# A one-core AdaLN attention and MoE-LoRA block: VectorE's rsqrt of the second FFN half's rows taken apart over units, row statistics ahead of row scalings, two mask banks exchanged

## What is computed

```python
sa, ca, ga, sb, cb, gb = mod(c)                     # six rows per batch
h = layernorm(x) * (1 + ca) + sa
x = x + ga * attn(h)          # attn: layernorm(h)*gamma+beta, q k v, causal softmax, o_proj, + h
h = layernorm(x) * (1 + cb) + sb
x = x + gb * ffn(h)

# ffn
gate_base, up_base = xf @ Wg.T, xf @ Wu.T           # 704 columns each
probs = softmax(xf @ Wr.T); top 2 of 8 experts per row
base_out = (silu(gate_base) * up_base) @ Wd.T
for each expert e, for the rows that picked it:
    h = silu(gate_base + xf @ Ag_e.T @ Bg_e.T * 2) * (up_base + xf @ Au_e.T @ Bu_e.T * 2)
    acc += w_e * (h @ Ad_e.T @ Bd_e.T * 2)
```

## Time and profile before

| what | value |
|---|---|
| time, median of 3 runs | 670.26 us (670.22 to 670.79) |
| profiled execution, its own time | 669.96 us |
| its span | 668.1 us |
| TensorE matmul (PE) busy | 652.1 us, 98% of the span |
| TensorE weight load (PEld) busy | 561.4 us, 84% |
| VectorE (DVE) busy | 466.5 us, 70% |
| ScalarE (ACT) busy | 360.3 us, 54% |
| GpSimd (POOL) busy | 369.5 us, 55% |
| granted TensorE clock, mean | 0.997 |

### The profile page before, as it was taken

One profiled execution on the slowest core, in us unless ns is written; L12 is line 12 of the kernel. 1 busy time (PEld: TensorE's weight loads), 2 busy tenths in 40 slices (PEclk: granted clock), 3 DMA queues, 4 the chain that ended last, 5 costly groups with the idle time before them and its releaser, 6 DMA issues.

```text
span 668.1 us, 10913 instructions
## 1 busy us (share of the span) xinstructions
PE 652.1 (98%) x3890; PEld 561.4 (84%) x3890; DVE 466.5 (70%) x1146; ACT 360.3 (54%) x646; POOL 369.5 (55%) x442
## 2 busy tenths in 40 slices
PE   8799999999999999999999999999999999999996
PEld 6488987888889987888889897887889998798885
DVE  5857676888785776688776677689886757547323
ACT  1766466545555547555455446564455456654543
POOL 1099366538658236657676317665666525633644
PEclk9999999999999999999999999999999999999999
DMA  8400020000000020000000001000000000000000
GB/s 308 138 1 1 2 64 0 1 1 32 0 1 32 1 65 1 0 1 33 0 1 32 1 6 59 1 1 33 1 0 27 7 1 1 1 1 1 32 0 33
DMA packets 15032, 15.47 MB, mean 23 GB/s; under 512 B 1793, under 2 KB 13697, under 8 KB 14977
## 3 DMA queue, kind: packets, MB, share of 16 engines
q1 hardware_dynamic: 14976, 14.76, 6.6%
HBM read 10.57 MB, written 4.19 MB: 22 GB/s over the span
## 4 chain that ended last, share of the span: by engine, by line
PE 84%; DVE 10%; ACT 3%; issue 1%; DMA 1%; POOL 0%; SPq 0%; DVEq 0%; ACTq 0%
PE ps L1265 78%; PE ps L1274 6%; DVE hid L1112 2%; DVE rstd L844 1%; DVE zb L864 1%; DMA xs<-in_L_attn_x 1%; DVE neg_mean L1176 1%; ACT xr L587 1%; ACT act_s L725 1%; DVE zb L867 0%; DVE stat L998 0%; DVE stat L861 0%; DVE topi L1057 0%; DVE xr L1007 0%; DVE nr_a L842 0%
## 5 line engine op out<-in xcount | busy, mean ns | idle before, releaser
L475 POOL TENSOR_TENSOR ring_lo<-hid,ring_hi 128x512 fp32r<-128x512 f32 x144 | 187.2, 1304 | 110.0 <-ACT ring_hi L733 109.4
L725 ACT ACTIVATE act_s<-ps 128x512 f32<-128x512 f32 x120 | 71.6, 597 | 123.0 <-PE ps L1265 122.4
L1112 DVE TENSOR_TENSOR hid<-act_s,ps 128x512 f32<-128x512 f32 x120 | 82.1, 684 | 78.9 <-ACT act_s L725 74.1
L733 ACT ACTIVATE ring_hi<-hid 128x512 fp32r<-128x512 f32 (+1 forms) x144 | 90.4, 627 | 5.3 <-PE ps L1265 3.5
L1265 PE MATMUL ps<-wdT_hi,ring_hi 128*128 128x256 f32 x192 | 53.2, 283 | 0.0
L1265 PE MATMUL ps<-wdT_lo,ring_hi 128*128 128x256 f32 x192 | 52.7, 280 | 0.0
L467 POOL TENSOR_TENSOR xT_lo<-tr_full,xT_hi 128x512 fp32r<-128x512 f32 x28 | 35.9, 1297 | 29.0 <-ACT xT_hi L597 29.0
L1265 PE MATMUL ps<-wdT_hi,ring_lo 128*128 128x256 f32 x160 | 44.7, 280 | 0.0
L1265 PE MATMUL ps<-vv_hi,pT_hi 128*128 128x256 f32 x144 | 42.9, 298 | 0.1
L1265 PE MATMUL ps<-tm_hi,bgT_hi 128*128 128x512 f32 x96 | 39.5, 411 | 2.4 <-DVE hid L1112 2.4
L482 POOL TENSOR_TENSOR xr<-xr,y_gb 128x256 f32<-128x256 f32 x31 | 22.6, 754 | 33.6 <-DVE y_gb L1147 33.6
(11 more groups left out here) (232 smaller groups left out, 2018.2 us busy)
## 6 DMA issues: line engine op xcount, KB each, us to landing
out<-xr SPq DMA_DIRECT2D x7, 512.0 KB, 2.9
xs<-in_L_attn_x SPq DMA_DIRECT2D x3, 1024.0 KB, 5.7
xs<-in_L_attn_x SPq DMA_DIRECT2D x2, 512.0 KB, 4.7
s_mod<-in_L_wmod SPq DMA_DIRECT2D x2, 512.0 KB, 7.6
s_qkvT<-in_L_attn_qkv SPq DMA_DIRECT2D x1, 768.0 KB, 7.4
wgT_raw<-in_L_ffn_Wg SPq DMA_DIRECT2D x1, 704.0 KB, 7.9
wuT_raw<-in_L_ffn_Wu SPq DMA_DIRECT2D x1, 640.0 KB, 8.7
wdT_raw<-in_L_ffn_Wd SPq DMA_DIRECT2D x1, 640.0 KB, 5.7
```

Source lines behind the costliest of these rows:

```text
L475: pool.tensor_sub(ring[1][:, place(n), :], hid[:, n % HID, :], ring[0][:, place(n), :].bitcast(fp32)).then_inc(h_lo.sem, 1)
L725: nc.scalar.activation(act_s[:, n % 2, :], ps[:, 2 * (n % 2), :], ACT.Silu).then_inc(silu_ready.sem, 1)
L733: nc.scalar.activation(ring[0][p0:P, place(n), :], hid[p0:P, n % HID, :], ACT.Copy).then_inc(h_hi.sem, 1)
L1112: V.tensor_mul(hid[:, n % HID, :], act_s[:, n % 2, :], ps[:, 2 * (n % 2) + 1, :]).then_inc(h_ready.sem, 1)
```

## The change

No instruction is added; VectorE's list gets two shorter per batch (`neg_mean` and `nr_h`).

- In the first half, the last row tile's statistics and `moments` go from behind r = 4 to behind r = 2. `guess` goes from behind r = 5 to behind r = 3 and no longer makes `nr_h`. The three Newton steps stand behind r = 4, 5 and 6, one each. `neg_mean` is dropped, and `shift` is made by one instruction from the mean and `rstd`.
- In the second half, `ln1_stats` stands ahead of `ln1_rows`.
- Mask 0 goes to bank 6 and mask 1 to bank 7, and TensorE waits for tile 6 ahead of mask 0 and for tile 7 ahead of mask 1.

```diff
-        MASK_BANKS = ((7, 6, 4, 5), (3, 4, 5, 6))
+        MASK_BANKS = ((6, 7, 4, 5), (3, 4, 5, 6))
...
-            def guess(lo, n, shifted=False):
+            def guess(lo, n, shifted=False, small=False):
...
-                mark(V.tensor_scalar(nr_h[:, lo:lo + n], v, -0.5, None, ALU.mult))
+                if not small:
+                    mark(V.tensor_scalar(nr_h[:, lo:lo + n], v, -0.5, None, ALU.mult))
...
-                    if r == 4:
+                    if r == 2:
                         x1_stats(TC + 3)
                         moments(range(TC, NT))
-                    if r == 5:
-                        mark(V.tensor_scalar(neg_mean[:, TC:NT], mv[:, TC:NT, 0], -1.0, None, ALU.mult))
-                        link(guess(TC, TC))
-                        rsqrt_steps(TC, TC, range(NEWTON - 1))
-                    if r == 6:
-                        rsqrt_steps(TC, TC, range(NEWTON - 1, NEWTON))
+                    if r == 3:
+                        link(guess(TC, TC, small=True))
+                    if 4 <= r < 4 + NEWTON:
+                        rsqrt_steps(TC, TC, (r - 4,))
+                    if r == 3 + NEWTON:
                         dve.sem_inc(norm_ready.sem, 1)
-                        V.tensor_mul(shift[:, TC:NT], neg_mean[:, TC:NT], rstd[:, TC:NT]).then_inc(rstd_ready.sem, 1)
+                        V.scalar_tensor_tensor(shift[:, TC:NT], mv[:, TC:NT, 0], -1.0, rstd[:, TC:NT], ALU.mult, ALU.mult).then_inc(rstd_ready.sem, 1)
...
+                        if 3 <= r < 3 + NT:
+                            ln1_stats(r - 3)
                         if 2 <= r < 2 + NT:
                             ln1_rows(b + 1, r - 2)
-                        if 3 <= r < 3 + NT:
-                            ln1_stats(r - 3)
...
-                pe.wait_ge(x1_ready.sem, x1_ready.at(b, NT - 1))
                 for m in range(2):
+                    pe.wait_ge(x1_ready.sem, x1_ready.at(b, NT - 2 + m))
                     pe.wait_ge(masks_spread.sem, masks_spread.at(b, 0))
                     mask(0, m)
```

More of the change, by code:

```diff
@@ L986, in _ @@
             setup_steps = steps[1]
-            VSTEPS = 102
+            VSTEPS = 100
             def body(b, last):
```

## The result

The changed kernel takes 672.9 us (median of 6 runs, 671.92 to 673.5), beside 670.51 for the kernel before (6 runs, 669.58 to 670.94). The ratio is 1.0038 (1.0026 to 1.005): 2.4 us slower. The forecast was 672.2, and its side was right.

The account below looks back on a forecast made before the run. TensorE, busy for 98% of the span, was taken as the bound, so only its starts count. Terms +4.2 - 1.2 - 1.0 = +2.0 on 669.96 us gave 671.9, carried to the median 672.2 us; range 667.4 to 674.7.

Parts of the forecast that it names:

- The guess behind r = 3: First FFN half: nr_v and rstd each wait for GpSimd, hidden(4) late, TensorE stands 1.79 us; net +1.04 us per batch.
- Who wins 0.06 us: Guess behind r = 3: GpSimd starts 0.05 ahead of nr_v and 0.06 ahead of rstd, deciding 1.3 us per batch.
- rival 1: The guess slips in ahead of hid_low(3), so TensorE stands only 0.69 us at unit 6; 667.8 us, chance 0.16.
- the equal case: The trace's same race at row 172.11: GpSimd starts 0.06 ahead of rstd, which then takes 1.25 us.
- Statistics and moments behind r = 2: First FFN half: they fit into VectorE's 1.14 us of idle time ahead of hidden(3); cost 0, at most 0.1.
- Newton steps behind r = 4 to 6: First FFN half: no collision behind r = 4, waits up to 1.3 us behind 5 and 6; cost 0, bound 0.3 per batch.
- Masks: The gap ahead of the masks goes, 0.21 to 0.32 us per batch, taken as 0.29; -1.2 us for four.
- Statistics ahead of scalings: Second FFN half: statistics hide in the scaling's wait for GpSimd, gaining 0.34 us three times; -1.0 us.
- rival 2: Behind r = 3 nr_v too wins its race, so no collision and no stall is left; 664.6 us, chance 0.06.
- rival 3: Late costs on top: hidden(7) or later scalings miss their room, or the masks' gain is lost; 674.3 us, chance 0.10.
- rival 4: The new TensorE stall of 1.8 us makes the clock fall, +6.8 us; 679 us, chance 0.03.
- rival 5: The moves change nothing on TensorE's path, or both signs cancel; within 0.2% of 670.3, chance 0.05.

Follow-up runs that it names:

- e5_low2_held: Changed kernel with one added wait: GpSimd starts hid_low(2) of the first FFN half only after hidden(4); 667.11 us, ratio 0.995.
- e6_low3_held: Changed kernel with one added wait: GpSimd starts hid_low(3) of the first FFN half only after hidden(4); 670.36 us, ratio 0.9999.
- e7_late_guess: Changed kernel with statistics and moments behind r = 4, guess and first Newton step behind r = 5, two steps behind r = 6; 666.85 us, ratio 0.9941.
- e2_masks_alone: Kernel before with only the two mask banks exchanged and the masks' waits made one by one; 669.42 us, ratio 0.9983.
- e3_stats_alone: Kernel before with only the statistics put ahead of the scalings in the second FFN half; 669.34 us, ratio 0.9976.
- e4_masks_stats: Kernel before with the mask change and the statistics ahead of the scalings, rsqrt as before; 668.4 us, ratio 0.9969.

## Why the prediction was right

**The bound and the aim.** Right. Nothing but TensorE's starts counted: VectorE had 1.0 us less to do and the kernel became slower.

**The guess behind r = 3.** Right in mechanism and size. `nr_v` was to take about 1.27 and took 1.22, `rstd` 1.27 and took 1.23; TensorE was to stand for 1.79 and stood for 1.75; the slow second start of 0.11 came as well. It is the term that decides: +1.04 forecast per batch, 1.75 + 0.11 - 0.75 - 0.11 = +1.00 found. `e5_low2_held` shows the cause rather than argues it: with the same VectorE instructions and GpSimd's one moved, the gap is gone.

**Who wins 0.06 us.** The forecast had GpSimd ahead by 0.05 and by 0.06; it was ahead by 0.10 and by 0.06 to 0.07, in all four batches, through a shift of some 1.1 us of the whole stage. The outcome was right, the reason only in part. It was that both engines hang on the same silu and shift together. But `hidden(3)` started behind the moments (its 0.33 of idle time end with `mv`), which set `nr_v` 0.05 further behind. `rstd` is no later for it, since `nr_v` ends with GpSimd's instruction whenever it started. And GpSimd's two starts are 1.50 apart before and after (95.94 and 97.44, 97.01 and 98.51). So the second race goes by GpSimd's own two starts.

The price on the other side of the race is as rival 1 had it (0.69 forecast, 0.70 in `e6_low3_held`). The race that the forecast held up as the equal case did turn. In the changed kernel `rstd` of the second half starts at 173.57 and takes 0.17, and GpSimd comes 0.27 behind it, at 173.84. It is so in batches 0 to 2 of every kernel with the statistics ahead of the scalings, and in none of the others; TensorE gained nothing by it. So two engines that shift together at one meeting need not do so at the next.

What the Trainium skill says on the page "SBUF — State Buffer", section "SBUF: two separate sides", that whoever starts first holds the shared port pair for the whole instruction, fits every pair of rows here. It also answers what the forecast left open, who is next: in `e5_low2_held` GpSimd's second instruction started 0.09 ahead of VectorE's, and won.

**Statistics and moments behind r = 2.** Taken as 0, at most 0.1. `hidden(3)` starts 96.51 - 95.38 = 1.13 later than before, 1.06 of it the span's scatter, so 0.07.

**Newton steps behind r = 4 to 6.** Right: none collided behind r = 4, those behind r = 5 and 6 took 0.94 and 1.21, and none cost TensorE anything. It was closer than the forecast's words: `hidden(7)` ends at 107.42 + 0.67 = 108.09 and unit 9 starts at 108.20, 0.11 later, of which some 0.05 is the way from `hidden` to TensorE (100.53 to 100.58 at unit 6). The bound of 0.3 a batch was worth keeping: `e7_late_guess`, with one step more there, has a gap of 0.54.

**Masks.** The mechanism right, the size 0.08 a batch too large: 0.21 found and 0.29 taken. The step that failed is the guess that a slow second start might stand behind the masks too; the distance behind them did not change.

**Statistics ahead of scalings.** Right: 0.37 fell to 0.06, 0.31 where 0.34 was taken; and no scaling met a new GpSimd instruction at a place where TensorE waits.

**Not foreseen:** the 0.23 in the second half of batch 1. It also stands, at the same instruction, in each of the five experiments that have the change's rsqrt in some form, and in none of the three that have the old one. It comes from a race that turned the other way. VectorE and GpSimd before (both scalings together, then the second by itself), and after (the second scaling by itself):

```profile
290.87 2.29 DVE L867 SCALAR_TENSOR_TENSOR zb<-xs,mv,bc 128x256 f32<-128x256 f32 x2
291.61 1.55 DVE L867 SCALAR_TENSOR_TENSOR zb<-xs,mv,bc 128x256 f32<-128x256 f32 x1
291.57 1.30 POOL L475 TENSOR_TENSOR ring_lo<-hid,ring_hi 128x512 fp32r<-128x512 f32 x1 [0.17 <-ACT ring_hi L733]
...
294.09 0.47 DVE L868 SCALAR_TENSOR_TENSOR zb<-xs,mv,bc 128x256 f32<-128x256 f32 x1
294.14 1.58 POOL L475 TENSOR_TENSOR ring_lo<-hid,ring_hi 128x512 fp32r<-128x512 f32 x1 [0.25 <-ACT ring_hi L733]
```

Before, the second scaling starts 0.04 behind GpSimd and takes 1.55. After, it starts 0.05 ahead and takes 0.47, and now GpSimd takes 1.58 in place of 1.30. What hangs on GpSimd is late in its turn: ScalarE's next three instructions, VectorE's from the first `xT_lo` on, and so TensorE. VectorE wins the race and the kernel loses 0.23. What moved this race is a `hidden` just before it (290.14 before, 292.70 after) that starts some 0.07 later against TensorE in all six kernels with the change's rsqrt; why it does is open.

**The sum.** By the gaps, 4 x 1.00 - 4 x 0.21 - 3 x 0.31 + 0.23 = +2.5, where the forecast summed to +2.0: the guess gives 0.16 less than forecast, the masks save 0.32 less, the statistics 0.09 less, and the new gap adds 0.23. The forecast of 672.2 is 0.7 under the measurement: some 0.5 by these four, and the kernel before measured 670.51 where 670.3 was taken. For the experiments the same count of gaps against the kernel before, in their order, gives +4.2, -0.8, -0.9, -1.8, -2.4, +0.6, -3.1 and -5.0 us, where the medians gave +4.0, -1.5, -1.6, -2.5, -3.5, -0.2, -3.7 and -5.5. The medians all lie lower, by 0.2 to 1.1 us. The profiled executions don't: from the first transposes behind the 3.8 us wait to the end, their differences are +4.6, -0.6, -1.2, -1.9, -2.6, +0.5, -3.4 and -5.1, within 0.4 of the count on either side (+2.5 for the change). So the gaps account for the profiled executions, and what lies on one side is mostly the yardstick. The profiled execution of the kernel before took 669.96, which is 0.6 to 1.0 below its medians beside the experiments, while those of the other nine kernels lie from 0.9 above theirs to 0.5 below. Of the expectations, those for `e5_low2_held` and `e6_low3_held` were 0.8 to 0.9 too high as times, and the gains of `e2_masks_alone`, `e3_stats_alone` and `e4_masks_stats` were expected 0.3 to 0.6 too small.

**Rivals.** Rivals 2, 3 and 4 did not come. Rival 1's race never turned, and rival 5's cancelling did not go so far. There was no clock loss: the 2 us around the stall and the 3 us behind it have a granted clock of 1.00, and in the other batches the 5 us that begin within the stall have it too (windows of the kernel after in batch 0; columns as in the earlier trace rows):

```profile
99.00:101.00 2.00, 0.42 (x2) 0.38 (x3) 1.89 (x5) 1.04 (x2) 0.78 (x1) 1.00 0.00 0
101.00:104.00 3.00, 3.00 (x15) 2.47 (x14) 1.88 (x4) 1.03 (x3) 1.29 (x1) 1.00 0.00 0
```

## What to carry to other kernels

An instruction of 0.17 us costs what it collides with, not what it does: before moving small SBUF-to-SBUF work on VectorE, lay the timelines of VectorE and GpSimd over each other and look at where each piece will start. The four batches repeat each other, so a race lost by 0.05 us is lost in every repetition. Nor is a race won for good: moves of a few hundredths to tenths of a us elsewhere turned two of them here, and one that VectorE won cost TensorE 0.23. So go through the later meetings of the two engines as well. Taking a chain apart over units gives it one chance of a collision per unit; here the same chain, begun in a unit where it meets one GpSimd instruction and not two, was worth some 6 us of 673 (`e7_late_guess` against the change).

## What was not expected of the hardware

- A chain of small instructions can be held twice in a row. Beside three GpSimd instructions that stood ready back to back (3.79 us for three), one took 1.29 and the next 1.22: by the time the first was done, GpSimd's next had started, 0.09 ahead.
- It works both ways. A scaling that started 0.05 ahead of a GpSimd instruction made that one 1.58 us long in place of 1.30.
- Holding GpSimd back by a wait made the changed kernel some 5.8 us faster, although GpSimd's results come later and four instructions of the chain are still held (1.29, 1.22, 0.60 and 0.69 us in batch 0 of `e5_low2_held`).
- A stall of TensorE of 1.75 us, four times, left the granted clock at 1.00, where one of 3.8 us is followed by 3.4 us at 0.50.
